# Issuing VectorE's operations over all node tiles in pieces of four tiles (graph network, one core)

## What is computed

```python
h = relu(layernorm(x));  x = x + relu(segment_sum(H_all[src, rel] * a, dst))   # L0, with edge_attr_64
h = relu(layernorm(x));  x = x + agg(relu(agg(h)))                             # L1, agg = segment_sum(h[src], dst)
h = relu(layernorm(x))                                                         # L2: four GCN convolutions
l1 = relu(gcn(h, W1, b1));  l2 = relu(gcn(l1, W2, b2))
td = relu(gcn(l2, W3, b3)) + l1;  x = x + relu(gcn(td, W4, b4)) + h
h = relu(layernorm(x))                                                         # L3
v_e = segment_sum(edge_attr_48, src) / max(count, 1)
out = x + relu(relu([h, v_e, u] @ W1 + b1) @ W2 + b2) @ W3 + b3
```

## Time and profile before

| | |
|---|---|
| time, median of 3 runs | 4679.84 us (4676.11 to 4682.98) |
| span of the profiled execution | 6104.5 us |
| own device time of the profiled execution | not given beside the span |
| busy, share of that span | PE 57%, POOL 52%, DVE 42%, ACT 25% |
| mean granted TensorE clock | 0.746 |

### The profile page before, as it was taken

One profiled execution on the slowest core, in us unless ns is written; L12 is line 12 of the kernel. 1 busy time (PEld: TensorE's weight loads), 2 busy tenths in 40 slices (PEclk: granted clock), 3 DMA queues, 4 the chain that ended last, 5 costly groups with the idle time before them and its releaser, 6 DMA issues.

```text
span 6104.5 us, 83728 instructions
## 1 busy us (share of the span) xinstructions
PE 3504.6 (57%) x18191; PEld 1755.8 (29%) x18192; DVE 2563.8 (42%) x7891; ACT 1503.7 (25%) x3741; POOL 3187.4 (52%) x3191
## 2 busy tenths in 40 slices
PE   5377777777777777776324544345365345455347
PEld 2133333333333333333101222112132112222136
DVE  6266666666666666666330020131120021120368
ACT  3133333323323232322211111111111112111158
POOL 2455555555555555555376555645625635626720
PEclk8588888878888887888656676667666667667679
DMA  5333333333333333333123444334324334324256
GB/s 181 93 77 81 81 78 78 77 80 77 77 77 80 77 77 78 80 77 71 38 93 135 145 146 131 119 112 145 107 79 144 111 132 146 108 79 156 79 200 237
DMA packets 593641, 646.86 MB, mean 106 GB/s; under 512 B 423668, under 2 KB 430418, under 8 KB 587261
## 3 DMA queue, kind: packets, MB, share of 16 engines
q1 hardware_dynamic: 374705, 459.40, 23.2%
q0 software_dynamic: 101760, 110.75, 9.2%
q10 hardware_dynamic: 117068, 75.50, 4.1%
HBM read 451.74 MB, written 190.23 MB: 105 GB/s over the span
## 4 chain that ended last, share of the span: by engine, by line
PE 35%; issue 21%; another core or an unknown queue 21%; DVE 10%; DMA 8%; ACT 2%; POOL 2%; DVEq 1%; SPq 0%; ACTq 0%; POOLq 0%
PE bank L1742 10%; PE bank L1743 7%; PE bank L1823 6%; PE bank L1747 6%; DMA ld_all<-adjacency 3%; DMA rel_table<-ld_all 2%; DMA rel_and_z<-adjacency 1%; DVE hid_T L1305 1%; DMA ld_all<-l_sorted 1%; POOL l_sorted L711 1%; DVE hid_T L1326 1%; DVE hid_T L1584 1%; PE bank L1939 1%; PE bank L1771 1%
## 5 line engine op out<-in xcount | busy, mean ns | idle before, releaser
L711 POOL DMA_INDIRECT l_sorted<-arena,l_pos x1504 | 1539.2, 1023 | 1339.3 <-ACT arena L854 877.4
L686 POOL DMA_INDIRECT ld_all<-rel_table,rel_and_z x1564 | 1545.8, 988 | 1133.0 <-remote 503.2
L1742 PE MATMUL bank<-hid_T 128*128 128x400 f16 x2346 | 965.7, 412 | 672.6 <-issue 539.8
L1743 PE MATMUL bank<-hid_T 128*128 128x384 f16 x2346 | 940.5, 401 | 44.3 <-issue 43.5
L1326 DVE TENSOR_SCALAR hid_T<-count_key,hid_T 128x400 f16<-128x400 int16 x2346 | 592.1, 322 | 754.5 <-remote 526.7
L1823 PE MATMUL bank<-rel_and_z,ld_all 128*128 128x512 fp8e4 (+1 forms) x1872 | 522.3, 414 | 602.9 <-issue 534.1
L1823 PE MATMUL bank<-ld_all 128*128 128x512 fp8e4 (+1 forms) x1950 | 511.4, 420 | 337.4 <-issue 138.4
L1747 PE MATMUL bank<-ld_all,arena 128*32 x4692 | 527.1, 250 | 123.3 <-issue 121.3
L1742 PEld LDWEIGHTS bank<-hid_T 128*128 x2346 | 255.9, 109 | 1157.3 <-issue 1153.9
L774 ACT CAST ld_all<-bank 128x400 fp8e4<-128x400 f32 x391 | 191.1, 489 | 1551.6 <-remote 999.7
L1266 DVE COPY accT<-bank 128x512 f32<-128x512 f32 (+1 forms) x78 | 51.1, 656 | 1215.4 <-remote 797.1
(11 more groups left out here) (289 smaller groups left out, 4103.0 us busy)
## 6 DMA issues: line engine op xcount, KB each, us to landing
ld_all<-adjacency SPq DMA_DIRECT2D x72, 1600.0 KB
rel_and_z<-adjacency SPq DMA_DIRECT2D x72, 1600.0 KB
l_sorted<-zeros SPq DMA_DIRECT2D x147, 424.0 KB
arena<-in_edge_attr SPq DMA_DIRECT2D x195, 256.0 KB
ld_all<-l_sorted SPq DMA_DIRECT2D x33, 1277.5 KB, 6.0
adjacency<-ld_all ACTq DMA_DIRECT2D x391, 100.0 KB
rel_table<-ld_all SPq DMA_DIRECT2D x49, 520.0 KB, 3.6
ld_all<-rel_table,rel_and_z POOLq DMA_INDIRECT x1564
```

The source lines that it names most:

```text
L686: pool.indirect_dma_start(ring[:, c % RING, 0:TW], None, rel_table, bass.IndirectOffsetOnAxis(ap=rel_i[:, c:c + 1], axis=0)).then_inc(s(f" ...
L711: pool.indirect_dma_start(l3_sorted, bass.IndirectOffsetOnAxis(ap=l3_pos[0:parts, n * SB_K + k:n * SB_K + k + 1], axis=0), rows16[q][0:par ...
L1742: pe.matmul(b0[:, 0:w0], low[:, 0:P], pair_hot[q % 2][:, k, 0:w0], start=k == 0, stop=k == CG - 1)
L1743: pe.matmul(b1[:, 0:GW - w0], low[:, P:2 * P], pair_hot[q % 2][:, k, 0:GW - w0], start=k == 0, stop=k == CG - 1)
```

## The change

A helper cuts an operation over the tiles into operations over four tiles, and returns the last one, so that a link or a semaphore stands on the last alone:

```diff
+PART = 4
+            stat = lambda t, at: t[:, at].unsqueeze(2).to_broadcast([P, at.stop - at.start, D])
+            def by_parts(op, tiles=NT):
+                for t in range(0, tiles, PART):
+                    ins = op(slice(t, min(t + PART, tiles)))
+                return ins
             def layernorm(n, to=h, squares=G):
                 link(v.reduce_sum(mean[:], x[:], axis=AX.X))
                 link(v.tensor_scalar(mean[:], mean[:], 1.0 / D, None, ALU.mult))
-                link(v.tensor_tensor(to[:], x[:], stat(mean), ALU.subtract))
-                link(v.tensor_tensor(squares[:], to[:], to[:], ALU.mult))
+                link(by_parts(lambda at: v.tensor_tensor(to[:, at, :], x[:, at, :], stat(mean, at), ALU.subtract)))
+                link(by_parts(lambda at: v.tensor_tensor(squares[:, at, :], to[:, at, :], to[:, at, :], ALU.mult)))
                 v.reduce_sum(var[:], squares[:], axis=AX.X).then_inc(s("var_ready"), 1)
                 v.wait_ge(s("std_ready"), n)
                 link(v.reciprocal(var[:], var[:]))
-                link(v.tensor_tensor(to[:], to[:], stat(var), ALU.mult))
-                ins = v.tensor_scalar(to[:], to[:], 0.0, None, ALU.max)
+                link(by_parts(lambda at: v.tensor_tensor(to[:, at, :], to[:, at, :], stat(var, at), ALU.mult)))
+                return by_parts(lambda at: v.tensor_scalar(to[:, at, :], to[:, at, :], 0.0, None, ALU.max))
...
-                link(v.tensor_copy(x16[:, :, 0:D], scaled))
+                link(by_parts(lambda at: v.tensor_copy(x16[:, at, 0:D], G[:, at, :]), SRC_T))
...
-            link(v.tensor_tensor(G[:], G[:], U[:], ALU.add))
+            link(add_to(G, U))
```

More of the change, by code:

```diff
@@ L1245, in split_rows @@
                 link(v.tensor_copy(scale_row[:], bank[7][:, 0:D]))
-                scaled = G[:, 0:SRC_T, :]
-                link(v.tensor_tensor(scaled, U[:, 0:SRC_T, :], scale_row[:].unsqueeze(1).to_broadcast([P, SRC_T, D]), ALU.mult))
-                link(v.tensor_copy(x16[:, :, 0:D], scaled))
-                link(v.tensor_tensor(x16[:, :, D:2 * D], scaled, x16[:, :, 0:D], ALU.subtract))
+                link(by_parts(lambda at: v.tensor_tensor(G[:, at, :], U[:, at, :], scale_row[:].unsqueeze(1).to_broadcast([P, at.stop - at.start, D]), ALU.mult), SRC_T))
+                link(by_parts(lambda at: v.tensor_copy(x16[:, at, 0:D], G[:, at, :]), SRC_T))
+                link(by_parts(lambda at: v.tensor_tensor(x16[:, at, D:2 * D], G[:, at, :], x16[:, at, 0:D], ALU.subtract), SRC_T))
                 link(v.memset(G[:, SRC_T:NT, :], 0))
@@ L1465, in _, with add_to @@
                     v.sem_inc(s("turn"), 1)
-            link(v.tensor_tensor(U[:], U[:], s12[:, :, 1:2].to_broadcast([P, NT, D]), ALU.mult))
-            link(v.tensor_tensor(G[:], G[:], U[:], ALU.add))
-            link(v.tensor_scalar(G[:], G[:], 0.0, None, ALU.max))
-            link(v.tensor_tensor(x[:], x[:], G[:], ALU.add))
+            def add_to(acc, part):
+                return by_parts(lambda at: v.tensor_tensor(acc[:, at, :], acc[:, at, :], part[:, at, :], ALU.add))
+            link(by_parts(lambda at: v.tensor_tensor(U[:, at, :], U[:, at, :], s12[:, at, 1:2].to_broadcast([P, at.stop - at.start, D]), ALU.mult)))
+            link(add_to(G, U))
+            link(by_parts(lambda at: v.tensor_scalar(G[:, at, :], G[:, at, :], 0.0, None, ALU.max)))
+            link(add_to(x, G))
             with v.If(flag2):
@@ L1498, in gcn_sum, with add_bias, relu_of @@
                 agg(j - 1)
-                link(v.tensor_tensor(G[:], G[:], U[:], ALU.add))
-                return v.tensor_tensor(G[:], G[:], stat(dinv), ALU.mult)
+                link(add_to(G, U))
+                return by_parts(lambda at: v.tensor_tensor(G[:, at, :], G[:, at, :], stat(dinv, at), ALU.mult))
+            def add_bias(acc, bias):
+                return by_parts(lambda at: v.tensor_tensor(acc[:, at, :], acc[:, at, :], bias[:].unsqueeze(1).to_broadcast([P, at.stop - at.start, D]), ALU.add))
+            def relu_of(acc):
+                return by_parts(lambda at: v.tensor_scalar(acc[:, at, :], acc[:, at, :], 0.0, None, ALU.max))
             def dense(n):
@@ L1535, in _ @@
             link(gcn_sum(4))
-            link(v.tensor_tensor(G[:], G[:], g_b2[:].unsqueeze(1).to_broadcast([P, NT, D]), ALU.add))
-            link(v.tensor_scalar(G[:], G[:], 0.0, None, ALU.max))
-            v.tensor_tensor(U[:], G[:], stat(dinv), ALU.mult).then_inc(s("u_ready"), 1)
+            link(add_bias(G, g_b2))
+            link(relu_of(G))
+            by_parts(lambda at: v.tensor_tensor(U[:, at, :], G[:, at, :], stat(dinv, at), ALU.mult)).then_inc(s("u_ready"), 1)
             gcn_sum(5).then_inc(s("late"), 1)
@@ L1541, in _ @@
             link(gcn_sum(6))
[L1542 to L1545, removed]
+            link(add_bias(G, g_b4))
+            link(relu_of(G))
+            link(add_to(G, h))
+            link(add_to(x, G))
             link(layernorm(5))
-            link(v.tensor_tensor(x[:], x[:], m_b3[:].unsqueeze(1).to_broadcast([P, NT, D]), ALU.add))
+            link(add_bias(x, m_b3))
             v.sem_inc(s("late"), 1)
```

10 lines of the change are left out of this document (4 added, 6 removed).

## The result

| | kernel before | with pieces |
|---|---|---|
| time, median | 4681.41 us (4676.11 to 4685.1, 4 runs) | 4598.41 us (4597.38 to 4601.6, 4 runs) |
| ratio, 95% interval | 1 | 0.9824 [0.981, 0.9838] |
| forecast | | 4626 us, 4585 to 4685 |

The change saves 83 us, 1.8%. Direction and mechanism came as forecast, and the time lies in the range; the saving is 29 us larger than the 54 us of the forecast.

The account below looks back on a forecast made before the run. GpSimd's scatters, held up by whole VectorE operations, were taken to be last for much of the second part. +3.3 - 68 + 11 = -54 us against the median 4679.8 gave 4626 us, range 4585 to 4685.

Parts of the forecast that it names:

- the missing 1425 us: Profiled span over the median: taken as mostly PE stalls at line 1823, absent from timed runs.
- GpSimd's 1929 us: Second part: its 1504 scatters, 1472 x 1.27 + 32 x 1.85 us, set a floor the part can't fall below.
- rival C: Second part: GpSimd last only at both ends, so the middle earns nothing; -6 us, 4674 us, chance 0.14.
- 101 us: Beside the scatters: GpSimd's loss to 40 two-source operations at 2.4 us and 8 one-source ones at 0.66.
- 33 us: Beside streams of pieces: GpSimd's remaining loss, 131 scatters at 0.25 us each.
- My lower end, 4593: Forecast if a scatter beside pieces loses 0 us: -87 us in all.
- +11 us: End of the two `dense` places, in `split_rows`: GpSimd empty, relief of 4 operations lost, 6 operations cost 0.8 us each.
- +3.3 us: Before the scatters: the first `layernorm` stands alone on the path, its pieces cost 3 x 0.8 + 0.9 us.
- A stream's length: VectorE: 13 two-source pieces take 4.42 us, starting 0.33 us apart; 13 one-source pieces take 2.8 us.
- The cast: Line 1248, 3136 elements in 3.42 us: its pieces taken at the same slow rate, +0.8 us.
- What the next profile was to show: Line 711's maximum under 1.6 us, last 32 scatters 50 to 58 us busy, VectorE ending before GpSimd, pieces 0.33 us apart.
- rival B: Beside the scatters: 13 pieces hold GpSimd as one operation does; +42 us, 4722 us, chance 0.07.

Follow-up runs that it names:

- tail alone in pieces: Changed kernel with pieces of four tiles only behind the sixth aggregation, everything else whole; 4659.07 us, ratio 0.9945.
- two-source alone: Changed kernel with only operations of two SBUF inputs cut; relu, copies and float16 rounding stay whole; 4606.56 us, ratio 0.9834.
- pieces of four, linked: Changed kernel with a link (semaphore and wait) behind every piece; 4647.79 us, ratio 0.9921.
- the earlier trace: Profile of the unedited kernel before, with PE's stalls, that the prediction was made from; span 6104.5 us.
- the first experiment: Kernel before, unedited, run again for a profile not stretched by PE's stalls; 4686.78 us, ratio 1.0007.
- The last four comparisons: Changed kernel with pieces of two, of one linked, of eight, or another last-block layout, on another chip: 6156.7, 6627.47, 6175.78, 6101.78 us beside 6068.33.
- pieces of four with the shorter last block: Changed kernel with the last block's rows over all 128 partitions, 27 scatters in place of 32; 6101.78 us beside 6068.33, ratio 0.9998.

## Why the prediction was right

| run | line 711/712 busy | lost to VectorE (busy - 1476.0) | waits for ACT | first to last scatter |
|---|---|---|---|---|
| before | 1599.4 | 123.4 | 30.2 | 2088.3 |
| tail alone in pieces | 1577.9 | 101.9 | 30.9 | 2068.1 |
| pieces of 13 | 1525.1 | 49.1 | 41.2 | 2024.4 |
| two-source alone | 1502.0 | 26.0 | 49.5 | 2009.8 |
| pieces of four | 1491.9 | 15.9 | 50.8 | 2001.5 |
| pieces of four, linked | 1495.4 | 19.4 | 88.9 | 2041.7 |
| pieces of one | 1691.7 | 215.7 | 38.7 | 2189.3 |

The last column is always the scatters' time, the waits and the gaps between them, so that it adds up proves nothing. What the rows show is that the gaps stay the same, that GpSimd waits for ACT in 30 to 89 us of some 2050 and is at its scatters in the rest, and that the kernel follows this stretch: from the start of the last scatter to the end of the span all seven runs take 263 to 267 us. The stretch and the start of the first scatter (2327 to 2343 us) make up the whole difference in their spans. That is the prediction's frame, GpSimd last in the second part with VectorE taking its time, and it held.

- **Where the missing 1425 us lie.** Right that the runs of 4680 us have no such stalls. But I took the 1936.5 us of the earlier trace rows for idle time of the products, and they count the weight loads (PEld) of line 1823 too. For the products alone the view gives:

```profile
  issue: 672.5, 354
```

In the first experiment it gives none; the 404.9 us of "issue" at this line are all weight loads there. 672.5 us can't be most of 1425. The first scatter starts at 3053.6 us with the stalls and at 2330.4 without, so half of the missing time, 723 us, lies in front of it, in the loop; there PE's products of lines 1742 and 1743 wait 583 us without a cause in place of 191, and are busy for 280 us more. So taking all 1425 us off the second part was far too much: without stalls it takes 2092.9 us to the first sorted load, not 1367, as against 2792 with them. The other bound, GpSimd's 1929 us, was the one that counted. I left open what carries the stalls. The last four comparisons show that it isn't the profiling: there the same kernel takes 6068 us when timed. That it is the chip is likely but not shown. PE's timeline in the run with pieces of two tiles is that of the earlier trace rows:

```profile
4207.00 0.59 PE L1840 MATMUL bank<-ld_all 128*128 128x512 fp8e4 x1 [2.21 <-issue]
4209.80 0.59 PE L1840 MATMUL bank<-ld_all 128*128 128x512 fp8e4 x1 [2.21 <-issue]
```

- **GpSimd last, and rival C.** Right where the forecast was made. Under the stalls something like C happens: GpSimd waits for ACT for 800 us and more in each of those traces, and pieces of four with the shorter last block gain nothing. Pieces of four alone weren't tried there.
- **"101 us" lost to whole operations: mis-sized.** It was 123.4. I priced every two-source operation at 2.4 us, the loss inside a run of them. One that stands alone holds the scatter beside it to 0.84 us behind its own end (4.27 us beside line 1499, for one that starts 0.20 us into it, so 3.3 lost), and a one-source operation right behind a two-source one adds to the same scatter (the 5.28 us above) or costs 1.4 us alone (2.34 beside line 1482), not 0.66.
- **"33 us" lost to pieces: mis-sized.** It was 15.9. I took 0.25 us for a scatter, the middle between 0 and 0.49; the scatters beside pieces show 0.06 (1.03 against 0.97), a few 0.2. The bounds held. What I drew them from was no test of the case, though: the six operations of line 1326 read one array each, and streams of one source hold nothing even in pieces of 64 elements (58 scatters start in them and take 1.03 us at most). That two-source pieces let scatters in was right by luck, for four tiles and not for one. My lower end, 4593, is 5 us from the result by luck too: GpSimd's losses to whole operations were 22 us larger than the sum has them, and 15.9 us of losses to pieces and 9.6 us more of waits, less the 3.3, take the same 22 us back.
- **"+11 us" where GpSimd runs dry: mechanism and places right, size off.** Waits for ACT grow by 20.6 us: 22.62 us at 3381.84 and 25.23 at 4022.99, behind the two `dense` places (13.21 and 16.95 before), and a third of 2.95.
- **"+3.3 us" of the first layernorm: wrong, about 0.** The pieces of its last operation even take 0.63 us each, and the first gather of the loop starts 6.9 us later (207.95 us for 201.09). But the last gather starts 1.1 us later, and the first scatter at 2329.5 us for 2330.4: the loop takes it up. I can't say why.
- **Together:** -107.5 + 20.6 = -86.9 us where the sum had -68 + 11 + 3.3 = -54. The spans differ by 85.8.
- **A stream's length.** 4.46 us forecast as 4.42, pieces 0.34 us apart against 0.33; one source 2.96 against 2.8. Right.
- **The cast.** I took the slow rate, wrongly. The pieces run at the fast one, as the rule of the Trainium skill (Vector Engine (DVE) Microarchitecture Reference, Performance modes) had it: 2.9 us for 13 in place of 4.2. The run with pieces of 13 tiles has both cases: its pieces of 13 tiles, an odd number, go at the slow rate, and the last piece of each cast, 10 tiles, at the fast one. Here are the casts of the changed kernel, and the two of that run:

```profile
L1253 DVE CAST ld_all<-G 128x256 f16<-128x256 f32 x72 | 16.4, 300 | 0.2
...
L1253 DVE CAST ld_all<-G 128x832 f16<-128x832 f32 x18 | 17.2, 1013 | 0.2
L1253 DVE CAST ld_all<-G 128x640 f16<-128x640 f32 x6 | 2.9, 483 | 0.0
```

- **What the next profile was to show.** VectorE still ends before GpSimd (4254 against 4332.6 us). The longest scatter is 2.9 us and not under 1.6: a single one, the first of all, held by the first stream as rival B has it; 8 of 1472 are over 1.2 us. The last 32 take 49.6 us, not because of the pieces, but because VectorE has ended before them, in the kernel before too.

## What to carry to other kernels

Where one engine's queue sets the pace, ask which instructions of the others hold it, and how long without a break; cutting those into pieces of 256 elements cost VectorE a quarter more time and gave GpSimd 107 us. Then try the sizes on both sides: here 832 elements gave back a quarter of the gain, and 64 made the kernel 2.4% slower than no pieces at all. Count how many pieces go by between two instructions of the other engine: four were fine here, seven mostly too many. And the same cut costs 23 us once the other engine is no longer last, so look at who waits at the end of each stage first, in a profile whose time is that of the timed runs.

## What wasn't expected of the hardware

A stream of unlinked two-source pieces lets a scatter in at 0.06 us as long as some six pieces at most have started since the last one; behind that it is held to 0.84 us behind the last piece. With 64 elements the stream is closed by 0.98 us after its start; with 256 it happened to one scatter of 118; with a link behind every piece nothing is held. Of the one-source streams those of 64 elements hold nothing. A rounding of 3136 elements in 3.42 us, a reduction of 3.62 us and operations with one of two inputs in PSUM hold nothing, while a one-source operation of 3328 elements in 1.89 us does. A scatter of 106 rows takes 1.55 us, one of 128 rows 0.97. And one and the same kernel took 4681 to 4684 us on two chips and 6068 on another, with PE waiting 2.21 us between products of 0.59.
